# Second and third attention of a four-block kernel: shared rows for PV and sums, fewer reciprocals, dense output products, reordered steps

## The reference

```python
# block 1 (latents x: 128 rows; h = context rows and latent rows, 256 in all)
q = (latents @ q_w + q_b).reshape(b, k_len, NH, DH)        # NH = 16 heads, DH = 16
kv = (h @ kv_w + kv_b).reshape(b, p + k_len, NH, DH, 2)
attn = softmax(where(full_mask, einsum('bkhd,bnhd->bhkn', q, kmat) / DH, -inf))
attn_out = einsum('bhkn,bnhd->bkhd', attn, v).reshape(b, k_len, H) @ out_w + out_b + residual
out = rmsnorm(attn_out, postnorm_w); return gelu(out @ mlp_w1 + mlp_b1) @ mlp_w2 + mlp_b2 + residual
# block 2: the same shape with layer norms, 128 keys, 16 heads of 16
```

## Time and profile before

| | |
|---|---|
| runs | 1220.92, 1221.82, 1226.72 us; median 1221.82 |
| profiled execution | 1221.06 us, span of its instructions 1219.3 us |
| mean granted TensorE clock | 0.947 |
| PE (TensorE matmul) | 991.2 us busy, 81% |
| PEld (weight load) | 612.9 us, 50% |
| DVE (VectorE) | 615.7 us, 50% |
| ACT (ScalarE) | 463.1 us, 38% |
| POOL (GpSimd) | 267.1 us, 22% |
| chain that ended last | PE 68%, DVE 21%, issue 7%, ACT 2% |

### The profile page before, as it was taken

How to read it: one execution, slowest core, us unless ns; L and a number is a source line. 1 busy time by engine, 2 the same in 40 slices (tenths; PEclk the granted TensorE clock), 3 DMA queues, 4 the chain that set the end, 5 groups by cost and what they waited for, 6 DMA issues and landing times.

```text
span 1219.3 us, 20340 instructions
## 1 busy us (share of the span) xinstructions
PE 991.2 (81%) x7888; PEld 612.9 (50%) x7888; DVE 615.7 (50%) x1263; ACT 463.1 (38%) x881; POOL 267.1 (22%) x386
## 2 busy tenths in 40 slices
PE   7888789897897878888798878979788887976672
PEld 6465444564454654555546644546535454444430
DVE  1444544555546654465455555465544555554431
ACT  1414244343442444344342424424343344422223
POOL 0311111142111510232111421115112231023103
PEclk9899999999999999999999999999989999998667
DMA  9200120010200111002200102001020012001001
GB/s 379 93 1 1 70 95 26 6 70 5 96 31 1 74 51 55 22 2 74 95 19 14 66 10 95 31 2 74 9 87 31 2 74 86 17 16 69 5 1 35
DMA packets 29054, 60.60 MB, mean 50 GB/s; under 512 B 9376, under 2 KB 21024, under 8 KB 24096
## 3 DMA queue, kind: packets, MB, share of 16 engines
q1 hardware_dynamic: 28960, 59.29, 13.3%
HBM read 54.04 MB, written 5.24 MB: 49 GB/s over the span
## 4 chain that ended last, share of the span: by engine, by line
PE 68%; DVE 21%; issue 7%; ACT 2%; POOL 1%; DMA 1%; DVEq 0%; SPq 0%; POOLq 0%; ACTq 0%
DVE nm L1358 7%; PE GP L956 5%; PE PV L702 5%; PE GP L564 5%; PE GP L965 5%; PE GP L566 5%; DVE U L1423 5%; PE SC L685 3%; PE SC L771 3%; PE GP L938 3%; PE GP L749 3%; PE GP L788 3%; PE SC L873 2%; PE MX L618 2%; PE GP L948 2%
## 5 line engine op out<-in xcount | busy, mean ns | idle before, releaser
L1358 DVE TENSOR_REDUCE nm<-MX 128x2 bf16<-128x512 f32 (+1 forms) x352 | 227.1, 689 | 203.1 <-PE MX L624 111.5
L1672 POOL TENSOR_TENSOR Psum<-Pr 128x512 f32<-128x512 f32 x56 | 70.9, 1266 | 294.4 <-ACT Pr L1164 294.4
L1166 ACT ACTIVATE Pr<-SC,bcol 128x512 f32<-128x512 f32 x128 | 81.1, 684 | 131.5 <-PE SC L771 131.5
L564 PE MATMUL GP<-zP,W 128*128 128x128 f32 x512 | 103.2, 284 | 6.9 <-DMA W<-w 6.9
L1191 ACT ACTIVATE Pr<-SC,bcol 128x512 f32<-128x512 f32 x96 | 60.8, 684 | 115.8 <-PE SC L873 115.8
L566 PE MATMUL GP<-uP,W 128*128 128x128 f32 x512 | 100.1, 277 | 0.0
L1164 ACT ACTIVATE Pr<-SC 128x512 f32<-128x512 f32 x128 | 69.3, 593 | 62.8 <-PE SC L685 62.8
L564 PEld LDWEIGHTS GP<-zP,W 128*128 128x128 f32 x512 | 79.8, 194 | 15.8 <-issue 13.6
L1646 POOL TENSOR_TENSOR stat<-stat,half 128x1 f32<-128x1 f32 x24 | 13.6, 565 | 326.9 <-DVE stat L1532 179.2
L566 PEld LDWEIGHTS GP<-uP,W 128*128 128x128 f32 x512 | 78.9, 195 | 0.0
L702 PE MATMUL PV<-Pr,V 128*64 128x256 f32 x512 | 75.6, 420 | 0.0
(11 more groups left out here) (184 smaller groups left out, 1709.0 us busy)
## 6 DMA issues: line engine op xcount, KB each, us to landing
WA<-w1a SPq DMA_DIRECT2D x8, 1024.0 KB, 6.0
WB<-w1b SPq DMA_DIRECT2D x8, 1024.0 KB, 8.1
WA<-w2a SPq DMA_DIRECT2D x8, 1024.0 KB, 5.0
WB<-w2b SPq DMA_DIRECT2D x8, 1024.0 KB, 7.1
W<-w SPq DMA_DIRECT2D x6, 1024.0 KB, 9.9
scratch<-U SPq DMA_DIRECT2D x16, 256.0 KB, 2.0
C<-scratch SPq DMA_DIRECT2D x96, 32.0 KB
zP<-z_in SPq DMA_DIRECT2D x8, 128.0 KB, 4.3
```

The source lines that it names most:

```text
L564: pe.matmul(dst, W0[:, piece, 2 * s, at:at + P], zP[:, s * P:s * P + P], start=True, stop=False)
L1166: act.activation(Pr[:, (n + j) % 4, :], SC[j], ACT.Exp, bias=bcol[:, 3 + k % 2:4 + k % 2], scale=8.0 ** -0.5).then_inc(p_ready, 1)
L1358: dve.tensor_reduce(dst, MX[(n + i) % 2][:].rearrange("p (a k) -> p a k", a=a), AX_X, ALU.max, negate=True).then_inc(mx_done, 1)
L1672: pool.tensor_tensor(Psum[:, c % 4, :].rearrange("p (a l) -> p a l", l=D), two[:, :, 0:D], two[:, :, D:2 * D], ALU.add)\
```

## The change

- V1 and V2 have a head's 16 values in slots of 32 columns, where the next 16 columns are zero; a view that begins 16 columns earlier has the values in the upper half. Of a pair of groups, the first fills rows 0 to 15 of each strip of 32 and the second rows 16 to 31, in the same PSUM columns, by accumulation. Four further products by `ones2` put the sums of weights, in the same way, into the next 128 columns of the bank.
- A quotient serves eight heads: one reciprocal of 128 x 128 and one product, and no shuffle. Two quotients instead of four, two dense output products instead of four (`pairs`), the columns of the value weights reordered (`heads`).
- A bank of PV for each pair of groups.
- In the second attention v1c and the transposes come before the second pair of maxima; qp0 before T on TensorE and after it on VectorE; `end3` before qp1; vp0 behind the last PV.
- In the third attention k3 comes behind the first scores; block 0's T and scores0 come before the output product.
- In the mixed passage ENTRY is spread over steps (0, 4) and (0, 5), which now both come before (3, 0).
- V3 has a tile of its own; W1O and W2O are half as large.

```diff
@@ -68,10 +68,10 @@
 BOTH = [(0, 0, [], []), (0, 1, [], []), (0, 2, [], []), (0, 3, [], []),
-        (0, 4, [], []), (3, 0, [], [(3, 1, 0)]), (3, 1, [], [(3, 1, 2)]), (0, 5, [(3, 1, "T")], [(0, 3, 0)]),
-        (3, 2, [], [(0, 3, 2)]), (3, 3, [(0, 3, "T")], [(3, 2, 0)]), (0, 6, [], [(3, 2, 2)]),
-        (0, 7, [(3, 2, "T")], [(3, 3, 0)]), (3, 4, [], [(3, 3, 2)]), (3, 5, [(3, 3, "T")], [(0, 0, "B")]),
-        (3, 6, [], [(0, 1, "B")]), (3, 7, [], [])]
+        (0, 4, [(3, 0, 0)], [(3, 0, 2)]), (0, 5, [(3, 0, "T")], [(3, 1, 0)]), (3, 0, [], [(3, 1, 2)]),
+        (3, 1, [(3, 1, "T")], [(0, 3, 0)]), (3, 2, [], [(0, 3, 2)]), (3, 3, [(0, 3, "T")], [(3, 2, 0)]),
+        (0, 6, [], [(3, 2, 2)]), (0, 7, [(3, 2, "T")], [(3, 3, 0)]), (3, 4, [], [(3, 3, 2)]),
+        (3, 5, [(3, 3, "T")], [(0, 0, "B")]), (3, 6, [], [(0, 1, "B")]), (3, 7, [], [])]
 FIRST = alone(0)
...
@@ -79,6 +79,10 @@
+def entry(b):
+    return ENTRY if b == B - 1 else []
 def mix_of(b):
...
@@ -96,7 +100,7 @@
             if (L, k) == (3, 0):
-                units(b, ENTRY)
+                units(b, entry(b))
             units(b, middle)
...
@@ -110,14 +114,14 @@
         more = b < B - 1
-        banks0(b, [("xT",), ("lat",)] + [(1, g) for g in range(NG)])
+        banks0(b, [("xT",), ("lat",), (1, 0), (1, 1)])
         units(b, UNITS1)
...
             banks0(b + 1, [("pv", 0)])
-        banks0(b, [(2, g) for g in range(NG)])
+        banks0(b, [(2, 0), (2, 1)])
         units(b, UNITS2)
...
-        Ax = sb("Ax", [P, NG, P])
-        junk3 = Ax[:, 0:2, :].rearrange("p g k -> p (g k)")
+        V3 = sb("V3", [P, 2, NH, 32])
+        Ax = sb("Ax", [P, 2, P])
+        junk3 = Ax[:].rearrange("p g k -> p (g k)")
         res1 = sb("res1", [P, D])
...
@@ -282,6 +287,11 @@
+        def values12(tile):
+            return tile[:, 0:34 * 16].rearrange("p (j y) -> p j y", j=2)[:, :, 0:D]\
+                .rearrange("p j (x c) -> p j x c", c=32)[:, :, :, 0:16]
         def A0(m):
...
@@ -400,7 +410,7 @@
                 return (s_hT if kind == "xT" else s_lat), b + 1
-            return s_Ax, 8 * b + 4 * (kind - 1) + which[0] + 1
+            return s_Ax, 4 * b + 2 * (kind - 1) + which[0] + 1
...
@@ -806,7 +816,7 @@
                     if (L, k) == (3, 0):
-                        for name in ENTRY:
+                        for name in entry(b):
                             unit(*name)
...
@@ -876,29 +887,30 @@
                     n = SC_AT[b, L, 2 * (halves * c + kc)]
+                    bank = pv_bank(b, L, c)
+                    if kc == 0:
+                        pe.wait_ge(*pv_bank_taken(b, L, c))
                     for r in range(2):
-                        g = 2 * c + r
-                        bank = pv_bank(b, L, g)
                         pe.wait_ge(p_ready, n + r + 1)
-                        if kc == 0:
-                            pe.wait_ge(*pv_bank_taken(b, L, g))
-                        for t in range(4):
-                            mm = pe.matmul(bank[32 * t:32 * t + 32, 0:P], V(HG * g + t, kc),
-                                           Pr[:, (n + r) % 4, t * P:t * P + P], start=(kc == 0),
-                                           stop=(kc == halves - 1), skip_group_check=True)
+                        for at, weights in ((0, lambda t: V(2 * c + r, t, kc)), (P, lambda t: ones2[:, r, :])):
+                            for t in range(4):
+                                mm = pe.matmul(bank[32 * t:32 * t + 32, at:at + P], weights(t),
+                                               Pr[:, (n + r) % 4, t * P:t * P + P], start=(at == kc == r == 0),
+                                               stop=(kc == halves - 1 and r == 1), skip_group_check=True)
                         mm.then_inc(pv_done, 1)
-                entry, then = (UNITS1[:4], [UNITS1[4:5], UNITS1[5:]]) if L == 1 else (UNITS2[:3], [UNITS2[3:]])
-                for _, g, u in entry:
-                    if (g, u) == (0, "T"):
-                        amid()
+                units = UNITS1 if L == 1 else UNITS2
+                cuts = (4, 5, 6) if L == 1 else (3, 4)
+                for _, g, u in units[:cuts[0]]:
                     make(g, u)
+                    amid(g, u)
                 steps = [(c, kc) for c in range(2) for kc in range(halves)]
...
                     scores(c, kc)
+                    before(i)
                     if i == 1:
                         pe.wait_ge(*v_ready)
-                    for _, g, u in (then[i] if i < len(then) else []):
+                    for _, g, u in (units[cuts[i]:cuts[i + 1]] if i + 1 < len(cuts) else []):
                         make(g, u)
...
@@ -939,13 +951,11 @@
-                def slots_out(name, W, which, between=None):
+                def slots_out(name, W, which):
                     g, full = begin(name)
-                    for s in range(NG):
-                        if s == 2 and between:
-                            between()
-                        pe.wait_ge(s_Ax, 8 * b + 4 * which + s + 1)
-                        mm = pe.matmul(g[:, 0:D], Ax[:, s, :], W[:, s, :], start=(s == 0), stop=(s == NG - 1))
+                    for s in range(2):
+                        pe.wait_ge(s_Ax, 4 * b + 2 * which + s + 1)
+                        mm = pe.matmul(g[:, 0:D], Ax[:, s, :], W[:, s, :], start=(s == 0), stop=(s == 1))
                     mm.then_inc(full, 1)
...
@@ -984,13 +994,16 @@
-                def amid1():
-                    wait(pe, *pv_bank_taken(b, "lat"))
-                    for c in range(2):
-                        mm = pe.transpose(pv_bank(b, "lat")[:, c * P:c * P + P], hT[:, c, P:D], ident[:])
-                    mm.then_inc(s_latT, 1)
-                    v1("v1c", 0)
-                    fill("qp0")
+                def amid1(g, u):
+                    if (g, u) == (0, 0):
+                        wait(pe, *pv_bank_taken(b, "lat"))
+                        for c in range(2):
+                            mm = pe.transpose(pv_bank(b, "lat")[:, c * P:c * P + P], hT[:, c, P:D], ident[:])
+                        mm.then_inc(s_latT, 1)
+                        v1("v1c", 0)
+                    if (g, u) == (0, 2):
+                        fill("qp0")
...
@@ -1004,9 +1017,14 @@
                         make03[0](0, 2 * (i - 2))
-                    if i in (1, 2):
-                        fill("qp1" if i == 1 else "vp0")
-                attention12(b, 1, make, K1, lambda h, kc: V1[:, kc, h, :], (s_V1, 2 * b + 2), amid1, after1)
+                    if i == 1:
+                        fill("qp1")
+                def slot(g, t):
+                    return 32 * (g % 2 * 8 + g // 2 * 4 + t)
+                attention12(b, 1, make, K1, lambda g, t, kc: V1[:, kc, slot(g, t):slot(g, t) + 32],
+                            (s_V1, 2 * b + 2), amid1, after=after1)
+                fill("vp0")
                 slots_out("o1", W1O, 0)
...
@@ -1037,19 +1055,20 @@
+                def before2(i):
+                    if i == 0:
+                        g, full = begin("k3", (ld_w3, 16))
+                        pe.matmul(g[:, 0:D], W3[:, 1, :], uC[:], start=True, stop=True).then_inc(full, 1)
                 def after2(i):
-                    if more and i == 0:
-                        make03[0](1, 2)
+                    if more:
+                        make03[0](1, "T" if i else 2)
                 make = maxima_pass(b, 2, K2b, b2row[:], [(s_K2b, b + 1)])
-                attention12(b, 2, make, K2, lambda h, kc: V2[:, h, :], (s_V2, b + 1), lambda: fill("vp3"), after2)
-                g, full = begin("k3", (ld_w3, 16))
-                pe.matmul(g[:, 0:D], W3[:, 1, :], uC[:], start=True, stop=True).then_inc(full, 1)
-                def between2():
-                    if more:
-                        make03[0](1, "T")
-                        scores0(b + 1, 2)
-                slots_out("o2", W2O, 1, between2)
+                attention12(b, 2, make, K2, lambda g, t, kc: V2[:, slot(g, t):slot(g, t) + 32], (s_V2, b + 1),
+                            lambda g, u: fill("vp3") if u == 0 and g == 0 else None, before2, after2)
+                if more:
+                    scores0(b + 1, 2)
+                slots_out("o2", W2O, 1)
                 if more:
...
@@ -1278,12 +1297,16 @@
                 fill("vp2", "vp3")
-                attention12(b, 2, 0.25)
-                g = take(o, "k3")
-                for e in range(2):
-                    ins = act.activation(K3[:, e, :], g[:, 0:D], ACT.Identity, scale=hmask[:, 8 + e:9 + e],
-                                         bias=col("bkm", e))
-                ins.then_inc(s_K3, 1)
+                def keys3(i):
+                    if i != 1:
+                        return
+                    g = take(o, "k3")
+                    for e in range(2):
+                        ins = act.activation(K3[:, e, :], g[:, 0:D], ACT.Identity, scale=hmask[:, 8 + e:9 + e],
+                                             bias=col("bkm", e))
```

(78 more changed lines are left out.)

## The result

| | before | changed |
|---|---|---|
| median of the runs (us) | 1223.36 | 1100.87 (1099.8 to 1101.53) |
| ratio | | 0.8996, 95% interval 0.8971 to 0.9022 |
| profiled execution, span (us) | 1221.06, 1219.3 | 1099.8, 1098.0 |
| mean granted clock | 0.947 | 0.970 |
| mean of seven full batches (us) | 142.98 | 126.89 |

The direction and the places were right, the size was not.

A forecast was written before the change was run, and what follows sets the result against it. In-order TensorE was taken as the bound, losing time to VectorE waits in three places and to clock falls. Seven periods at 14.6 give 102.2, less 1.6, plus 3.2: 103.8 us saved, so 1118; range 1105 to 1144.

The forecast's parts named there:

- second attention up to xa: Second attention: new orders, shared quotients and separate PV banks let VectorE take xa at 531.1 instead of 535.72, gaining 4.6 us.
- third attention up to the next block's PV: Third attention: waits for quotients go and scores0 covers the last one; 6.3 us at the product, 6.2 behind the next PV's wait.
- entry of the mixed passage, q3 to the maxima: Entry to mixed first and fourth attention: bare waits of 1.58 and 1.56 us get filled; gain 3.9 us, 1.7 from clock.
- The cross-check: Whole period, by account: idle 17.5 less what is left, plus 3.3 of clock, less 1.6 added TensorE work, giving 14.5 us.
- the walks: Three stretches of a full batch, orders followed with traced durations: gains of 4.6, 6.2 and 3.9, together 14.7 us a period.
- The time by the page, 1149: PV steps: the skill's 81 ns per load-and-multiply pair makes the 96 added records cost 7.8 us a period, not 3.4.
- rival (c): PV steps: the doubled PV is dearer than its form; twice the price adds 24 us, so 1142; chance 0.07.
- rival (d): More gain than walked, from the last batch's clock and shrinking short waits: 1 to 2 us a period, 1103 to 1110; chance 0.12.
- rival (a): The three stretches: the clock keeps falling as long as now, 23 us come back, so 1141; chance 0.13.
- Moving `end3`: Second attention: C's reciprocal, 1.60 us, between qp1 and the first quotient, moves ahead of qp1, where VectorE has nothing else.
- k3's move: Third attention: k3 goes from behind it into the wait for the second maxima; 1.22 us before, 0.46 at full clock.
- What is late next is TensorE itself: Second attention after the change: TensorE becomes the late engine, with about 1.5 us of short waits left.

## Why the prediction was wrong in size

The bound, the three places and the releasers were read rightly. Step by step, for batch 3 where a row is meant:

| step | forecast | measured |
|---|---|---|
| second attention up to xa | 4.6 | 5.3 |
| third attention up to the next block's PV | 6.2 | 6.55 |
| entry of the mixed passage, q3 to the maxima | 3.9 | 4.4 |
| a PV step of 32 records | 1.14 | 1.01 |
| reciprocal of 128 columns out of PSUM | 0.96 | 0.95 |
| idle time of TensorE gone in a batch | 12.8 | 12.6 |
| busy time of TensorE gone in a batch | 1.7 | 3.85 |
| seven full batches | 100.6 | 112.7 |
| last batch | 3.2 | 9.75 |

**Two terms of the sum failed.** Together they are 18.6 us; less the 1.1 us of the longer prologue, that is the 17 that were missing.

The first is the priced gain of a full batch, 14.4 us where 16.1 came, short by 1.7 us a batch and 12 in seven. What was mis-sized in it is TensorE's own work: 119 to 120 us busy forecast, 117.2 measured. The cross-check, which was to confirm the walks, took the idle time right and the busy time wrong. Of the missing 2.15 us of batch 3, 0.8 is the PV step: the forecast doubled 0.57, but a step of 16 records is two packs at 0.22 each with a fixed part of 0.13 that comes once a step, so 32 records take 0.13 + 4 x 0.22 = 1.01. The run with the ones twice shows the 0.22. The Trainium skill (TensorE: Matmul & The Clock Gate, Back-to-back issue gap) puts a load and its multiplication of 128 columns at about 81 ns; here eight records on column strips in 0.22 us are 28 ns each. The time by the page, 1149, is 48 us above the measured one, and rival (c), the dearer PV, fell with it. The rest I read from the rows, no run tests it: a product that waits leaves its whole length in the trace, one that follows another only its distance to it. Records of 0.39 us follow each other at 0.22:

```profile
501.24 0.39 PE L574 MATMUL GP<-zP,W 128*128 128x128 f32 x2
501.46 0.39 PE L576 MATMUL GP<-uP,W 128*128 128x128 f32 x2
```

So each gap that closes gives about 0.17 us more than its idle time, and 27 gaps became 18: some 1.5 us, an estimate. The output product shows it best: two products by themselves are 0.70 each in the earlier trace rows, and the four records together 1.03. The forecast priced them at 0.456 a product on both sides, 0.9 us gained; in the second attention the output product was busy for 1.13 + 0.70 + 0.70 = 2.53 us before and is for 1.03 now, 1.5 gained, which is part of the 1.5 of the gaps. The walks went by starts and hold this partly, and they too were short, by 0.35 to 0.7 us each. Their waits were not the reason: they left 1.5, 1.7 and 1.5 us, and the trace has 1.6, 1.3 and 2.2, the last 0.7 more than was allowed at the entry.

The second is the last batch, 6.5 us. The forecast said that two serial quotients at the end of an attention become one. That is so where other work lies between the first pairs of groups. In the third attention of the last batch nothing does, and in the trace of before all four stood in a row. VectorE before, then after:

```profile
1137.27 0.16 DVE L425 TENSOR_TENSOR gate<-half 128x1 f32<-128x1 f32 x1 [3.97 <-PE PV L886]
...
1143.49 0.29 DVE L1424 TENSOR_TENSOR Ax<-PV,U 128x128 f32<-128x128 f32 x1
```

```profile
1024.75 0.16 DVE L435 TENSOR_TENSOR gate<-half 128x1 f32<-128x1 f32 x1 [2.56 <-PE PV L897]
...
1027.07 0.29 DVE L1440 TENSOR_TENSOR Ax<-PV,U 128x128 f32<-128x128 f32 x1
```

6.5 us have become 2.6, so 3.9 and not 1.7. The row was there to be read; I had looked only at xa. And the next MLP, which ran at the lower clock before, ran at the higher one:

```profile
1158.71 6.67 PE L965 MATMUL GP<-WB,work 128*128 128x256 f32 x16 [2.87 <-DVE work L1461]
```

```profile
1041.01 3.69 PE L975 MATMUL GP<-WB,work 128*128 128x256 f32 x16 [2.87 <-DVE work L1477]
```

3.0 us there. The forecast had no term for the clock of the last batch in its sum; it named it in rival (d), with 0.12 and 1103 to 1110, which the result passed as well. In the second attention of the last batch, on the other hand, only 0.6 of the forecast 1.5 us came; the mean granted clock up to xa is 0.88 there now, where it was 0.94. 3.9 + 3.0 + 0.6 = 7.5; the other 2.2 of the 9.75 us I have not put to a place. That the clock of this batch has a price at all is shown by the run with the useless products, 4 us of the last batch; the split of the 9.75 us is only read from two traces, and in the other kernels its length moved by a few us, and the places where the clock fell moved too.

**Steps that held.** No PV waits for a quotient; the output products run without a gap; the clock is at 1.00 in every full batch, so rival (a), 1141, fell; v1c and qp0 were worth the 1.54 us of the walk (+1.59 when undone), and vp0 still covers the last quotient (+1.26). The first batch gained 14.9 where the other six gained 16.3 in the mean, 1.4 less: the forecast said 1.6, for the C it has not to invert. k3 takes 0.5 us (512.87 to 513.41).

**Right total, wrong reason in a part.** Moving `end3` was a numbered step of the walk; undone, it costs 0.00. The reason holds for the order before, where the first quotient came at once, but with a quotient that now waits 1.65 us for PV, the reciprocal of C is covered in either place. k3's move was argued as a filler of a wait; in the traced execution it is worth 0.06, for it fills one of two waits of about equal length (0.42 and 0.50). "What is late next is TensorE itself" fell: with 3.8 us more on VectorE a batch is 3.14 us longer. The trace says the same, with 9.9 us of idle time left in a batch, about half of it ended by VectorE's maxima and the copies of their shifts.

**Where the 121 us come from.** Of the 16.1 us a batch, the entry holds 4.9 and the four orders 2.9, both measured by undoing them. What stays, 8.3 us, belongs to the shared rows, the two quotients instead of four, the banks of their own and the place of T and scores0 in the third attention. These weren't run one by one. Whether the sum comes from the shared rows, from fewer quotients or from the banks is therefore not shown. The granted clock runs through all of them: a full batch before had 6.8 us at the lower level (10.2 in one of the seven), 3.4 us lost, seven times about 24 us. The entry alone gives none of it back in the trace, and with everything but the entry 3.4 to 6.8 us a batch stay. The four orders are not needed for it: with all of them undone, six of seven full batches have no fall.

## What to carry to other kernels

Where an engine runs in order, price a closed gap by the distance of starts, not by idle time plus mean durations: a pipelined record costs its spacing, here 0.22 us where the record shows 0.39, and a fixed part counts once a step. Treat the granted clock as one account for the whole loop: as long as other gaps stay, closing one may only move the fall. Not every gap has to go: waits of 1.56 and 0.95 us put back into the second attention of the changed kernel left the clock at 1.00. Which gaps matter, no run here sorts out. Read the first and the last pass of a loop by themselves, instruction by instruction, since what hides a cost inside the loop is missing there.

## What the runs showed of the hardware

- A pack of four FP32 products of 32 columns, each on its own column strip with 128 columns to move, takes 0.22 us, whether its weights are values or ones; doubled, 0.44.
- A fall of the granted clock that filled gaps took from one place came back in another: 6.8 us at 1.2 GHz in six of seven batches before, and in five of seven after filling. The changed kernel has none in a full batch, and none either with waits of 1.56 and 0.95 us put back.
- Work that computes nothing shortened the last batch by 4 us (136.2 to 132.2 us) as it raised the clock of its third attention from 0.78 to 0.96.
- A reciprocal of 128 columns takes 0.95 us out of PSUM as out of SBUF, one of 256 columns 1.73.
